# Selective scan on one core: state sums kept in turned form, four of sixteen B products moved to ScalarE

## The reference

```
x  = silu(causal_conv4(x_in) + conv_b)               # per channel
dt, B, C = split(x_proj_w @ x)                       # 16, 16, 16 rows
dt = softplus(dt_w @ dt + dt_b)
h[d,n] = exp(dt[d] * A[d,n]) * h[d,n] + dt[d] * x[d] * B[n]     # over time
y[d]   = sum_n h[d,n] * C[n]  +  D[d] * x[d]
```

## Time and profile before

| | us |
|---|---|
| median of three executions | 8392.82 |
| profiled execution | 8391.64 |
| its span | 8389.9 |
| VectorE busy | 7255.9 |
| TensorE busy | 7633.5 |
| ScalarE busy | 5015.7 |
| GpSimd busy | 3693.2 |
| scan stage, first scan to last copy of y | 2612.5 to 5959.6 |

### The profile page before, as it was taken

One profiled execution on the slowest core, in us unless ns is written; L12 is line 12 of the kernel. 1 busy time (PEld: TensorE's weight loads), 2 busy tenths in 40 slices (PEclk: granted clock), 3 DMA queues, 4 the chain that ended last, 5 costly groups with the idle time before them and its releaser, 6 DMA issues. The chain is left out here.

```text
span 8389.9 us, 132293 instructions
## 1 busy us (share of the span) xinstructions
PE 7633.5 (91%) x40012; PEld 3197.5 (38%) x40012; DVE 7255.9 (86%) x10619; ACT 5015.7 (60%) x7151; POOL 3693.2 (44%) x1326
## 2 busy tenths in 40 slices
PE   6999999989988888888889999898889999999899
PEld 3333333325543333333333333333553333333355
DVE  6988888858877999999999999999658888888588
ACT  3577777773255666566666666666316777777622
POOL 0010000110015999999999999999510001101000
PEclk9899999999999999999999999999988999999999
DMA  6101101112263222222233333333670001010121
GB/s 178 18 19 20 20 19 20 19 33 68 73 205 115 86 84 84 84 84 84 84 95 94 96 95 92 95 93 95 203 223 16 19 20 20 20 27 13 37 80 60
DMA packets 532315, 605.82 MB, mean 72 GB/s; under 512 B 195520, under 2 KB 344768, under 8 KB 527616
## 3 DMA queue, kind: packets, MB, share of 16 engines
q1 hardware_dynamic: 527104, 564.73, 22.8%
q0 software_dynamic: 4608, 33.56, 2.0%
HBM read 399.85 MB, written 163.69 MB: 67 GB/s over the span
## 5 line engine op out<-in xcount | busy, mean ns | idle before, releaser
L833 DVE TENSOR_REDUCE ffn_att_mx<-psum 128x1 f32<-128x512 f32 (+3 forms) x4608 | 2725.7, 652 | 357.2 <-PE psum L674 204.1
L794 ACT ACTIVATE ffn_att_e<-psum,unscale 128x1024 f32<-128x1024 f32 (+3 forms) x2560 | 2376.8, 985 | 756.5 <-PE psum L739 750.5
L1695 POOL TENSOR_TENSOR scan_h<-scan_h,scan_cs 128x2048 f32<-128x2048 f32 x512 | 2334.8, 4626 | 228.1 <-ACT scan_state L1871 228.1
L1779 PE MATMUL psum<-scan_h,ident 128*128 128x512 f32 x4096 | 1961.5, 624 | 108.1 <-POOL scan_h L1695 108.0
L1998 DVE TENSOR_TENSOR_SCAN scan_h<-psum,scan_state,scan_db 128x512 f32<-128x512 f32 x1408 | 1677.4, 1261 | 10.6 <-ACT psum L1911 10.6
L641 POOL TENSOR_SCALAR_AFFINE_SELECT ffn_att_e<-ffn_att_e 128x512 f32<-128x512 f32 x512 | 324.6, 634 | 3012.3 <-ACT ffn_att_e L794 3012.3
L674 PE MATMUL psum<-ffn_att_k,ffn_att_q 48*128 48x512 f16 (+3 forms) x5120 | 1435.6, 367 | 174.7 <-DMA ffn_att_v<-v 59.2
L705 PE MATMUL psum<-ffn_att_e,ffn_att_v 128*32 128x512 f32 (+3 forms) x10240 | 1238.1, 556 | 8.1 <-ACT ffn_att_o L809 2.6
L1779 PEld LDWEIGHTS psum<-scan_h,ident 128*128 128x128 f32 x4096 | 795.6, 199 | 1176.6 <-issue 1038.5
L1911 ACT ACTIVATE psum<-scan_dt,scan_anr 128x512 f32<-128x512 f32 x1024 | 700.0, 686 | 542.5 <-DVE scan_h L1998 542.2
L1911 ACT ACTIVATE psum<-scan_dt,scan_anf 128x512 f32<-128x512 f32 x1024 | 699.8, 686 | 534.5 <-DVE scan_h L1998 533.9
(11 more groups left out here) (252 smaller groups left out, 7319.9 us busy)
## 6 DMA issues: line engine op xcount, KB each, us to landing
scan_cs<-scan_bcd SPq DMA_DIRECT2D x520, 256.0 KB, 3.1
scan_bs<-scan_bcd SPq DMA_DIRECT2D x162, 256.0 KB, 3.4
scan_win<-xp SPq DMA_DIRECT2D x34, 1036.0 KB, 7.0
scan_dt<-scan_sp POOLq DMA_DIRECT2D x32, 1024.0 KB, 6.9
mamba_out_ffn_in_ys<-both SPq DMA_DIRECT2D x18, 1024.0 KB, 7.7
mamba_out_ffn_in_zt<-zs SPq DMA_DIRECT2D x18, 1024.0 KB, 10.6
scan_yi<-y SPq DMA_DIRECT2D x17, 1024.0 KB, 6.7
ffn_att_q<-q_parts SPq DMA_DIRECT2D x128, 128.0 KB, 2.9
```

What stands on the lines that cost most here:

```text
L794: nc.scalar.activation(E[:, s % PB, 2 * hp:2 * hp + 2, off:CH], psum[:, 2 * hp:2 * hp + 2, off:CH], ACT.Exp, scale=unscale[:, 0:1]).then_i ...
L833: nc.vector.reduce_max(mx[:, hh * 2 + pairs[0]:hh * 2 + pairs[1], i // HALF, i % HALF, c // TT], psum[:, turn, 0:(pairs[1] - pairs[0]) * w ...
L1695: nc.gpsimd.tensor_tensor(h[n % NH][:, :, :], h[n % NH][:, :, :], cs[:, n % NCS, :].unsqueeze(1).to_broadcast([P, DM, CH]), ALU.mult).then ...
L1779: ins = nc.tensor.matmul(psum[:, m, :], ident[:, :], h[n % NH][:, m, :], start=False, stop=n == DS - 1)
```

## The change

Three things go together.

1. The sums are kept turned. Banks 0 to 3 now hold y by blocks t of 128 time steps (time in the partitions, all 512 channels in the columns). `sum_state` transposes h block by block into them and accumulates, 16 instructions with `is_transpose`; skip is laid out likewise. Forward y is stored in rows. In the reverse half the sum of both directions is turned back (`back`) through bank 7, kept by ScalarE (`keep_back`) in `sp1`, and stored from there.
2. Four B products per chunk, those of states 2, 5, 11 and 14 (`TURN_N`), are made by ScalarE. With time in the partitions, B[n] is one value per partition: TensorE turns dt*u once per chunk (`turn_du`), ScalarE keeps it in `duT` (`keep_du`), multiplies it by the column of B as the scale of a copy (`times_b`) into `bdu`, and TensorE turns each block back (`turn_back`) into the two decay banks. For these states ScalarE writes the decays to SBUF (`dec`), and the scan takes its decay from SBUF and its product from PSUM.
3. GpSimd makes the products of states 4, 7, 10 and 13; VectorE those of 0, 1, 3, 6, 8, 9, 12 and 15. Conv runs as whole steps at n = 7 to 10 and silu at n = 14.

```diff
-    NH, NCS = 4, 8
-    POOL_N = (3, 6, 9, 12, 15)
-    DVE_N = [n for n in range(DS) if n not in POOL_N]
+    NH, NCS, DBUF = 4, 8, 2
+    POOL_N, TURN_N = (4, 7, 10, 13), (2, 5, 11, 14)
+    DVE_N = [n for n in range(DS) if n not in POOL_N + TURN_N]
...
-    PE_X, PE_TURN, PE_DT, PE_CONV, PE_Y, SP_Y = 0, 2, 3, 7, 9, 11
-    A_SPLIT, A_TURN, A_SOFT, A_EXP, A_LN, A_SILU = 1, 3, 4, 8, 9, 15
+    PE_X, PE_TURN, PE_DT, PE_CONV, PE_Y, PE_BACK, PE_DU, SP_Y, SP_BACK = 0, 2, 3, 7, 9, 11, 14, 11, 14
+    A_SPLIT, A_TURN, A_SOFT, A_EXP, A_LN, A_SILU = 1, 3, 4, 8, 9, 14
...
                 def sum_state(i, n):
                     pe.wait_ge(hc_ready, DS * i + n + 1)
-                    for m in range(DM):
-                        ins = nc.tensor.matmul(psum[:, m, :], ident[:, :], h[n % NH][:, m, :], start=False, stop=n == DS - 1)
+                    for t in range(TT):
+                        for m in range(DM):
+                            ins = nc.tensor.matmul(psum[:, t, m * P:(m + 1) * P], h[n % NH][:, m, t * P:(t + 1) * P], ident[:, :],
+                                                   start=False, stop=n == DS - 1, is_transpose=True, skip_group_check=True)
...
+                def turn_back(i, n, m):
+                    k = DM * n + m
+                    if m == 0:
+                        pe.wait_ge(bdu_sb, du_count(i, n) // DM * TT + TT)
+                    pe.wait_ge(scanned, UNITS * i + k - 1)
+                    for t in range(TT):
+                        ins = nc.tensor.transpose(psum[:, BANK_A + k % 2, t * P:(t + 1) * P], bdu[:, t, m * P:(m + 1) * P], ident[:, :])
+                    ins.then_inc(db_ps, 1)
...
                 def step(i, par, first, opens, ends, way):
                     for n in range(DS):
-                        if (n + 1) % DS not in POOL_N:
+                        if n in TURN_N:
+                            for m in range(DM):
+                                turn_back(i, n, m)
+                        if (n + 1) % DS in DVE_N:
                             next_row_b(*chunk_of(i, par, n + 1))
...
+                def times_b(i, par, n, t, first):
+                    if t == 0:
+                        act.wait_ge(duT_sb, TT * (i + 1))
+                        act.wait_ge(bT_sb, i + 1)
+                        if not (first and n == TURN_N[0]):
+                            act.wait_ge(db_ps, du_count(i, n))
+                    nc.scalar.activation(bdu[:, t, :], duT[:, t, :], ACT.Copy, scale=bT[par][:, t, n:n + 1]).then_inc(bdu_sb, 1)
...
+                        kept = dec[k % 2][:, :] if n in TURN_N else psum[:, BANK_A + k % 2, :]
+                        nc.scalar.activation(kept, dt[par][:, m, :], ACT.Exp, scale=an[way(0)][:, m, n:n + 1]).then_inc(decay, 1)
...
+                        if n + 2 in TURN_N and m == 3:
+                            times_b(i, par, n + 2, 0, first)
+                        if n + 1 in TURN_N and m < 3:
+                            times_b(i, par, n + 1, m + 1, first)
+                        if (n, m) in ((12, 0), (12, 3), (13, 1), (13, 3)) and way(-1):
+                            keep_back(i - 1, ((12, 0), (12, 3), (13, 1), (13, 3)).index((n, m)), 2)
+                        if (n, m) in ((14, 3), (15, 0), (15, 2), (15, 3)):
+                            keep_du(i + 1, ((14, 3), (15, 0), (15, 2), (15, 3)).index((n, m)))
...
                         flip = FLIP[way(0)]
+                        ring = psum[:, BANK_A + k % 2, flip]
+                        if n in TURN_N:
+                            dve.wait_ge(db_ps, du_count(i, n) + m + 1)
+                            a_t, b_t = dec[k % 2][:, flip], ring
```

More of the change, by code:

```diff
@@ L1609, in store @@
                 def store(i, rev):
-                    hold(sp, y_read, DM * (i + 1), sp_passed)
-                    sp.dma_start(cols((y, both)[rev], place(i, rev)), yo[:, :, :]).then_inc(stored, 16)
+                    if rev:
+                        hold(sp, y_back, DM * (i - N + 1), sp_passed)
+                        sp.dma_start(cols(both, place(i, True)), sp1[:, :, :]).then_inc(stored, 16)
+                    else:
+                        hold(sp, y_read, TT * (i + 1), sp_passed)
+                        sp.dma_start(rows(y, place(i, False)), yo[:, :, :]).then_inc(stored, 16)
                 def store_bc(i, par):
@@ L1647, in step @@
                             store_bc(i + 1, 1 - par)
-                        if n == 3 and not first:
+                        if n == (SP_BACK if way(-1) else 3) and not first:
                             store(i - 1, way(-1))
@@ L1758, in next_row_b @@
                     after = n + 1
-                    while after % DS in POOL_N:
+                    while after % DS not in DVE_N:
                         after += 1
@@ L1812, in step @@
                             dt_proj(i + 1, n - PE_DT, way(1))
-                        if PE_CONV <= n < PE_CONV + 2 * DM:
-                            conv(i + 2, (n - PE_CONV) // 2, (n - PE_CONV) % 2, way(2))
+                        if PE_CONV <= n < PE_CONV + DM:
+                            conv(i + 2, n - PE_CONV, way(2))
+                        if PE_BACK <= n <= PE_BACK + 2 and way(-1):
+                            back(i - 1, (0, 1, 3)[n - PE_BACK])
+                        if n >= PE_DU:
+                            if n == PE_DU and way(-1):
+                                pe.wait_ge(y_back, DM * (i - N))
+                            elif n == PE_DU:
+                                pe.wait_ge(cv_sb, DM * (i + 3))
+                            turn_du(i + 1, 1 - par, 2 * (n - PE_DU))
                         if n == LAG:
@@ L1822, in step @@
                             sum_state(i - 1, DS + n - LAG)
+                        if n == PE_BACK + 1 and way(-1):
+                            back(i - 1, 2)
+                        if n >= PE_DU:
+                            turn_du(i + 1, 1 - par, 2 * (n - PE_DU) + 1)
                 in_steps(pe, step)
@@ L1825, in _ @@
                     sum_state(M - 1, n)
+                pe.wait_ge(duT_sb, TT * (M + 1))
+                for m in range(DM):
+                    back(M - 1, m)
             @block.scalar
@@ L1857, in softplus_in @@
                         act.wait_ge(dt_added, 16 * (i - 1))
+                        if not (isinstance(i, int) and i == 2):
+                            act.wait_ge(stored, 16 * (i - 2))
                     nc.scalar.activation(sp1[:, m, :], psum[:, bank, :], ACT.Abs, bias=tb[rev][:, m:m + 1]).then_inc(dt_read, 1)
@@ L1896, in _ @@
                 nc.scalar.activation(an[1][:, :, :], an[1][:, :, :], ACT.Exp).then_inc(a_exp, 1)
+                for t in range(TT):
+                    keep_du(0, t, t)
                 act.wait_ge(a_neg, 2)
@@ L2290, in macaron_block @@
     xp = scratch("xp", (DI, B, S + 2 * HALO))
-    zs, y, both = (scratch(n, (DI, NT)) for n in ("zs", "y", "both"))
+    zs, both, y = scratch("zs", (DI, NT)), scratch("both", (DI, NT)), scratch("y", (NT, DI))
     with ExitStack() as ctx:
```

112 lines of the change are left out of this document (80 added, 32 removed).

## The result

The changed kernel takes 8427.89 us (median of 7 executions, 8422.53 to 8448.5), the kernel before 8389.59 beside it (7, 8381.56 to 8410.95): ratio 1.0046, 95% interval 1.0036 to 1.0056. It is slower by 38 us, where I forecast no change. The profiled execution has a span of 8420.8 us, 31 more than before.

What follows compares the result with a forecast made beforehand. VectorE was taken to set the scan's pace. Chunks forward -1.9 and reverse +1.7 us, times 16 each, gave -3; loops -5, start +2, end +4: in all -2, forecast 8391 us, no change, range 8285 to 8500.

Steps and rivals of the forecast that it cites:

- my sum: Scan stage: 101.7 us per chunk forward, 105.3 reverse, together -3 us; the loops' extra time shrinks, -5 us.
- Removed, 7.0 us: Scan, per chunk: VectorE's products go from 11 to 8, 3 x 2.34 = 7.0 us less.
- State 1, ScalarE 0.5: State 1: ScalarE's scale copy and its copy of x_proj's result delay the scans by 0.5 us per chunk.
- the second rival: Rival, 23%: TensorE's low clock slows the kernel; at state 1, where ScalarE's copy waits for x_proj, 1.2 us.
- State 4, 2.4: State 4, per chunk: ScalarE's delay 1.1 us, and TensorE's late sum of state 0 at low clock 1.3.
- States 9 to 11, 2.3 and 4.9: Forward and reverse: ScalarE's delays at 9 and 10, 1.6 us; TensorE late at 11, 0.7 forward, 3.3 reverse.
- Silu 1.5: State 14: ScalarE's silu, with no conv output ahead of it, stalls 1.5 us in place of 1.9.
- Reverse states 12 to 14, 1.0: Reverse half, states 12 and 13: ScalarE's kept copies of y beside scale copies cost 1.0 us.
- states 6 to 8: State 6: Abs and Relu on ScalarE delay the scans by 0.4 us per chunk.
- TensorE's order costs nothing: Rival, 25%: chunks of 99.4 and 100.4 us, 8275 us; with half of the TensorE terms 8330.
- Low clock in the busy places: Rival, 23%: idling in turn_back puts conv and x_proj at low clock: 8538 us; in one chunk of three, 8440.
- Transposes keep the clock low: Rival, 7%: TensorE stays at the low clock throughout, +11.9 us per chunk, 8772 us.

Runs made afterwards that it cites:

- experiment 2: The changed kernel with x_proj ahead of the next row of B in state 0: 8412.21 us, 1.0032 to the kernel before.
- experiment 14: Only the four B products on ScalarE, sums, skip, other y and stores as in the kernel before: 8606.53 us, 1.0254 to that kernel.
- experiment 4: Only the turned sums, B products as in the kernel before (none on ScalarE): 8433.34 us, 1.0052 to that kernel.
- experiment 3: The changed kernel with half of skip's instructions before the third and fourth turn_back of state 2: 8382.10 us, 0.9989 to the kernel before.
- experiment 15: The changed kernel plus 16 transposes nobody reads, ahead of turn_back in state 2: 8399.12 us, 1.0006 to the kernel before.
- experiment 1: The changed kernel with the other direction's y added in state 11 instead of 9: 8403.45 us, 1.0018 to the kernel before.
- experiment 5: The changed kernel, other direction's y added in state 11 and the DMA adding sp1 into dt one state earlier: 8395.77 us, 1.0004 to the kernel before.
- experiment 11: 16 transposes nobody reads ahead of turn_back in state 2, added to a further edited changed kernel (8347.79 us): 8318.41 us, 0.9916 to the kernel before.
- experiment 8: The changed kernel with plain matmuls instead of transposes for the sums: 8648.75 us, 1.0304 to the kernel before.

## Why the prediction was wrong

The scan grew from 3336.5 us (first scan to last) to 3357.3: +21 where my sum had -8 (-3 by chunks, -5 by loops). The rest of the +31: the start 3 earlier (I had +2), the end 5 longer (I had +4), and 8 in later stages, whose code is the same: from the last scan to the end it is 2441 to 2465 us over the profiles of all kernels here, so I give it to no step. The start, too, differs between these profiles, 2597 to 2615 us, so 3 us there mean nothing.

- **Removed, 7.0 us:** right. It is why 5.7 us more of loss forward still leave a chunk 1.3 shorter.
- **State 1, ScalarE 0.5: the step that failed.** I took x_proj at 3.44 us and left its clock to the second rival ("1.2 at state 1"). It runs at the low clock in 28 chunks, ScalarE's copy of it waits, decays queue behind: 1.2 at state 2 forward, 1.1 reverse. 0.65 x 32 = 21 of the 29 us that the scan is off. Two things show it: the loss follows x_proj's end chunk by chunk, and where x_proj comes early and fast (experiment 2) 0.5 is left at state 2. I had the row in hand, 3.66 us of idle time at a chunk's end, and placed its low stretch at state 4 only. In the changed kernel the idle time stands right ahead of the row of B and x_proj. Neither half of the change does this alone: with the products alone (experiment 14) it is 2.1 to 2.2 us there in most chunks and x_proj is slow in 13 chunks, with the sums alone (experiment 4) mostly 0.4 to 1.5 us and 17 chunks.
- **State 4, 2.4:** right in size (2.5, 2.75), in part by luck: TensorE's term, forecast 1.3, was 1.9 and 2.2, ScalarE's, forecast 1.1, was 0.56, since its delay fell into TensorE's; without TensorE's wait it was 1.2 (experiment 3). The cause was right, by experiment 15: order 9.4 us at the full clock and nothing to spare, the loss is the clock. In the loops 6 chunks of 20 lost 3.2 at its start, which I did not have.
- **States 9 to 11, 2.3 and 4.9:** right as a sum (2.4, 5.0), with add_other as the cause of the 2.6 more in reverse (experiment 1). That its removal would pay in full was wrong: under it lay the wait for the DMA (experiments 1, 4, 5), which I never priced, because I looked at the copies' lengths and not at what sp1 waits for.
- **Silu 1.5:** 1.7. **Reverse states 12 to 14, 1.0:** 0.3 at 13 and 0.6 more than forward at 14. Both about right; states 6 to 8 lost 0.4 to 0.6 more than forecast. Some 0.2 of it comes from 9 chunks where dt projections ran at the low clock (2.07 us instead of 1.12) and state 7 lost 1.15 to 1.3 in place of 0.5; the rest was not followed.
- **The rivals.** "TensorE's order costs nothing" was false. "Low clock in the busy places" came nearest (8440 in one chunk of three), but its number is near by luck: at state 1 about half of its 1.2 was paid in nearly all chunks, at state 4 about its price in 6, at conv nothing. "Transposes keep the clock low" is false. TensorE does only transposes (a sum, turn_back, a row, turn_du) in these three stretches of the changed kernel, and its clock rises from 0.50 to 1.00:

```profile
4132.00:4136.00 4.00, 3.81 (x18) 3.81 (x19) 3.97 (x4) 3.27 (x7) 4.00 (x2) 0.50 0.28 66
4136.00:4140.00 4.00, 2.81 (x17) 2.18 (x16) 3.36 (x3) 3.97 (x3) 4.00 (x2) 0.73 0.00 0
4140.00:4144.00 4.00, 3.35 (x29) 2.88 (x27) 3.08 (x3) 3.03 (x6) 4.00 (x2) 1.00 0.28 66
```

The Trainium skill, "TensorE: Matmul & The Clock Gate", Part 4 (PE-mode transpose), says that they do not count as activity; the figure that stands beside it there is of bf16 transposes. For the fp32 ones here, and in experiments 11 and 15, the measurement decides against it.

Left open: why the added transposes help in only half of the chunks of kernel 15, and what the later stages' 24 us of scatter hang on.

## What to carry to other kernels

When an edit shortens TensorE's work, look where its idle time goes. Here what followed 3.8 us of idle time mostly ran near half speed (x_proj 5.3 to 6.1 us for 3.6), and where another engine waited for it, the gain was given back. An order without the gap gained 16 us, useless work in it 29. A copy into a shared buffer costs what the buffer waits for, not its length. And a wait seen was more than its removal paid (42 us seen and 24 paid in experiment 1, 66 and 46 in experiment 3): ask which one is hidden under it.

## What was unexpected

Sixteen transposes more per chunk made the kernel 29 us faster, twice. A state added by fp32 transposes takes 16 instructions and 1.9 us, by plain matmuls of the same shapes 32 and 3.7 us (experiment 8). The turned sums alone cost as much as the whole change (8433 and 8428), the products alone far more (8607): with the sums still 3.4 us long TensorE's order makes VectorE wait, so the products need the turned sums.
